# Row maxima of two heads in one instruction over two PSUM banks, with the diagonal's masks added by TensorE

## The reference

```python
scores = jnp.einsum('bqhd,bkhd->bhqk', Q, K) / math.sqrt(D_K)
causal = jnp.tril(jnp.ones((Sx, Sx), dtype=bool))
scores = jnp.where(causal, scores, -jnp.inf)
attn = jax.nn.softmax(scores, axis=-1)
out = jnp.einsum('bhqk,bkhd->bqhd', attn, V)
```

## Time and profile before

| | us |
|---|---|
| median of 3 runs | 2504.02 |
| lowest, highest | 2492.83, 2504.38 |
| the profiled execution | 2510.96 |
| its span, first to last instruction | 2509.3 |

### The profile page before, as it was taken

The page is one execution under the profiler, slowest core; times in us unless marked ns, Lnnn a source line. Parts: engine busy times, 40 slices in busy tenths (PEclk is TensorE's granted clock), DMA queues, the critical chain, the costliest instruction groups (busy, mean ns, idle before and its releaser), DMA issues. The chain is left out here.

```text
span 2509.3 us, 45515 instructions
## 1 busy us (share of the span) xinstructions
PE 2314.4 (92%) x16105; PEld 1323.9 (53%) x16105; DVE 1893.4 (75%) x5752; ACT 1516.1 (60%) x3189; POOL 505.8 (20%) x403
## 2 busy tenths in 40 slices
PE   5996999999999999999999999999957788999994
PEld 3553444444444444444444444444426688999994
DVE  3544988989989899899989988998707764666672
ACT  2541577778777778787777777787841102454451
POOL 0000001010110110101100100101005113777773
PEclk9996799989989899899989998998987787999997
DMA  5996405425244154253351551641117323666653
GB/s 166 295 243 194 57 5 70 52 36 70 37 52 61 19 75 54 29 70 43 45 70 26 63 61 19 78 52 28 15 34 223 127 84 103 141 132 136 143 124 85
DMA packets 145316, 214.56 MB, mean 86 GB/s; under 512 B 54560, under 2 KB 108000, under 8 KB 136672
## 3 DMA queue, kind: packets, MB, share of 16 engines
q1 hardware_dynamic: 132832, 195.27, 39.4%
q0 software_dynamic: 12288, 16.79, 5.2%
HBM read 138.43 MB, written 76.02 MB: 85 GB/s over the span
## 5 line engine op out<-in xcount | busy, mean ns | idle before, releaser
L654 ACT ACTIVATE probs<-s_banks 128x512 f32<-128x512 f32 (+3 forms) x2560 | 1184.6, 539 | 359.1 <-PE s_banks L605 200.6
L691 DVE TENSOR_REDUCE rowmax<-m_banks 128x1 f32<-128x512 f32 x1536 | 965.6, 682 | 87.5 <-PE m_banks L616 80.4
L605 PE MATMUL s_banks<-qs,ks 50*128 50x512 f32 (+3 forms) x2560 | 866.4, 437 | 15.7 <-ACT probs L654 9.5
L616 PE MATMUL m_banks<-ks,qs 48*128 48x512 f32 (+3 forms) x2560 | 830.6, 448 | 26.2 <-PEq L89 20.5
L634 PE MATMUL v_bank<-probs,vs 128*32 128x512 f32 (+3 forms) x5120 | 637.8, 572 | 1.0 <-ACT probs L654 0.4
L605 PEld LDWEIGHTS s_banks<-qs,ks 50*128 50x128 f32 x2560 | 422.2, 193 | 400.6 <-ACT probs L654 366.7
L616 PEld LDWEIGHTS m_banks<-ks,qs 48*128 48x128 f32 x2560 | 414.7, 197 | 297.3 <-DVE rowmax L691 137.5
L688 DVE CUSTOM_DVE_ANT_0 unused<-m_banks,c_maskq 128x128 bf16<-128x128 f32 (+3 forms) x1024 | 464.6, 486 | 81.1 <-issue 77.7
L551 POOL CAST nparts<-negmax 128x16 fp32r<-128x16 f32 x64 | 12.6, 197 | 1279.5 <-DVE negmax L697 1279.5
L1402 PE MATMUL e_banks<-w_parts,hid_parts 128*128 128x256 f32 x1536 | 188.8, 284 | 1.2 <-issue 0.5
L1402 PEld LDWEIGHTS e_banks<-w_parts,hid_parts 128*128 128x128 f32 x1536 | 185.4, 192 | 1.9 <-DVE hid_parts L1321 1.1
(11 more groups left out here) (181 smaller groups left out, 1823.8 us busy)
## 6 DMA issues: line engine op xcount, KB each, us to landing
w<-in_L_ffn_fc_w SPq DMA_DIRECT2D x32, 1024.0 KB, 5.2
qs<-q_scratch SPq DMA_DIRECT2D x96, 256.0 KB, 8.4
ks<-k_scratch SPq DMA_DIRECT2D x96, 256.0 KB, 10.2
q_scratch<-parts SPq DMA_DIRECT2D x64, 256.0 KB, 4.3
k_scratch<-parts SPq DMA_DIRECT2D x64, 256.0 KB, 4.5
v_scratch<-vt SPq DMA_DIRECT2D x16, 512.0 KB, 7.5
v_in<-v_scratch SPq DMA_DIRECT2D x32, 256.0 KB, 10.9
qs<-mrows SPq DMA_DIRECT2D x512, 2.0 KB
```

Source lines behind the costliest of these rows:

```text
L605: ins = pe.matmul(bank, ks[rows, slot, h // 2, k * P:(k + 1) * P], qs[rows, slot, h // 2, q * CH + first:(q + 1) * CH], start=True, stop=n ...
L616: pe.matmul(room(("M", NM * group + n))[:, 0:width], qs[rows, slot, h // 2, t * P:(t + 1) * P], ks[rows, slot, h // 2, c * CH:c * CH + wid ...
L654: act.activation(probs[:, n % PR, 0:width], s_banks[:, (NS * group + n) % SRING, 0:width], ACT.Exp, scale=SCALE).then_inc(p_ready, 1)
L691: dve.tensor_reduce(out, scores, AX.X, ALU.max).then_inc(m_used, 1)
```

## The change

The ring of four banks becomes a ring of two pairs: `m_banks` is [128, 2, 2, 512], `MRING` is 2, and a unit "M" is now the two blocks of the two halves that follow each other in `ROW_BLOCKS` (same rows, same columns, two heads). `group_order` appends a pair where it came to the second of its blocks. TensorE fills both banks, then on the diagonal adds the mask to each by two 64-column matmuls with an identity, as the score tiles do, and signals once. VectorE takes the maxima of both banks by one `tensor_reduce` with a [128, 2, width] input and a [128, 2] output, on the diagonal too; the masked instruction, its memset and `maskq` are gone. The transpose takes one of the two places of the ring (its first bank). Two bfloat16 tables come in, `later_row` and its copy with the halves swapped, with two more small DMAs.

```diff
--- before.py
+++ after.py
@@ -360,8 +360,8 @@
-            if group < G:
-                order.append(("M", group, n))
+            if group < G and n % 2 == 1:
+                order.append(("M", group, n // 2))
@@ -394,13 +394,14 @@
-MRING, SRING = 4, 3
+MRING, SRING = 2, 3
 ...
+    NP = NM // 2
@@ -411,7 +412,8 @@
-        ring.append(("M", block))
+        if block % 2 == 1:
+            ring.append(("M", block // 2))
@@ -434,10 +436,8 @@
-        unused = sb("unused", [P, GH, CH], BF16)
-        dve_pause = sb("dve_pause", [P, GH])
 ...
-        m_banks = ctx.enter_context(nc.psum_tensor("m_banks", [P, MRING, CH], F32))
+        m_banks = ctx.enter_context(nc.psum_tensor("m_banks", [P, MRING, 2, CH], F32))
@@ -581,7 +581,7 @@
-                while n >= 0 and ring[n][0] == "M" and ring[n][1] >= NM * G:
+                while n >= 0 and ring[n][0] == "M" and ring[n][1] >= NP * G:
@@ -608,16 +608,28 @@
-                        h, t, c = ROW_BLOCKS[n]
-                        width = min(CH, (t + 1) * P - c * CH)
 ...
-                        rows = slice(h % 2 * HALF, h % 2 * HALF + PAIR_ROWS)
-                        pe.matmul(room(("M", NM * group + n))[:, 0:width], qs[rows, slot, h // 2, t * P:(t + 1) * P],
-                                  ks[rows, slot, h // 2, c * CH:c * CH + width], start=True, stop=True).then_inc(m_ready, 1)
+                        banks = room(("M", NP * group + n))
+                        for half in range(2):
+                            h, t, c = ROW_BLOCKS[2 * n + half]
+                            width = min(CH, (t + 1) * P - c * CH)
+                            diagonal = c == t // TPC
+                            rows = slice(half * HALF, half * HALF + PAIR_ROWS)
+                            ins = pe.matmul(banks[:, half, 0:width], qs[rows, slot, h // 2, t * P:(t + 1) * P],
+                                            ks[rows, slot, h // 2, c * CH:c * CH + width], start=True, stop=not diagonal)
+                        if diagonal:
+                            for half in range(2):
+                                rows = slice(half * HALF, (half + 1) * HALF)
+                                for j in range(2):
+                                    mask = "later_row" if j == half else "later_row_swapped"
+                                    first = width - P + j * HALF
+                                    ins = pe.matmul(banks[:, half, first:first + HALF], const[mask][rows, :],
+                                                    const["identb"][rows, rows], start=False, stop=j == 1)
+                        ins.then_inc(m_ready, 1)
 ...
-                        bank = room(("N", turn))
+                        bank = room(("N", turn))[:, 0]
@@ -664,7 +676,7 @@
-                        act.activation(mrows[:, turn % 2, :], m_banks[0:PARTS * TILES, place[("N", turn)] % MRING, 0:P],
+                        act.activation(mrows[:, turn % 2, :], m_banks[0:PARTS * TILES, place[("N", turn)] % MRING, 0, 0:P],
@@ -678,20 +690,15 @@
-                        h, t, c = ROW_BLOCKS[n]
+                        h, t, c = ROW_BLOCKS[2 * n]
 ...
-                        out = rowmax[:, group % SLOTS, h % 2 * PAIRS + h // 2, t, c:c + 1]
-                        scores = m_banks[:, place[("M", NM * group + n)] % MRING, 0:width]
-                        dve.wait_ge(m_ready, NM * group + n + 1)
-                        if c == t // TPC:
-                            dve.memset(dve_pause[:, h:h + 1], 0.0)
-                            dve.tensor_tensor_reduce(unused[:, h, 0:width], scores, const["maskq"][:, CH - width:CH], 1.0, NEG,
-                                                     ALU.add, ALU.max, out).then_inc(m_used, 1)
-                        else:
-                            dve.tensor_reduce(out, scores, AX.X, ALU.max).then_inc(m_used, 1)
-                        if n in MAXIMA_ENDS:
-                            turn, q = NQ * group + MAXIMA_ENDS.index(n), t // TPC
-                            dve.wait_ge(m_used, NM * group + n + 1)
+                        out = rowmax[:, group % SLOTS, h // 2:h // 2 + PAIRS + 1:PAIRS, t, c]
+                        banks = m_banks[:, place[("M", NP * group + n)] % MRING]
+                        dve.wait_ge(m_ready, NP * group + n + 1)
+                        dve.tensor_reduce(out, banks[:, :, 0:width], AX.X, ALU.max).then_inc(m_used, 1)
+                        if 2 * n + 1 in MAXIMA_ENDS:
+                            turn, q = NQ * group + MAXIMA_ENDS.index(2 * n + 1), t // TPC
+                            dve.wait_ge(m_used, NP * group + n + 1)
@@ -1467,17 +1474,17 @@
-            for m in ("later_col",):
+            for m in ("later_col", "later_row"):
 ...
-            sp.wait_ge(swapped, 16 * 2)
+            sp.wait_ge(swapped, 16 * 4)
 ...
-            pool.memset(const["maskq"][:, :], 0.0)
+            pool.memset(const["later_row"][:, :], 0.0)
@@ -1493,8 +1500,8 @@
-            pool.affine_select(out=const["maskq"][:, CH - P:CH], in_=const["maskq"][:, CH - P:CH], compare_op=ALU.is_ge, fill=NEG, base=0,
-                               pattern=[[-1, P]], channel_multiplier=1).then_inc(made, 1)
+            pool.affine_select(out=const["later_row"][:, :], in_=const["later_row"][:, :], compare_op=ALU.is_ge, fill=NEG, base=0,
+                               pattern=[[1, P]], channel_multiplier=-1).then_inc(made, 1)
@@ -1524,9 +1531,9 @@
-                  "b1T": [P, E * F // P], "ident": [P, P], "upper": [P, P], "ones": [P, P], "eps": [P, 1], "maskq": [P, CH]}
+                  "b1T": [P, E * F // P], "ident": [P, P], "upper": [P, P], "ones": [P, P], "eps": [P, 1]}
 ...
-        for n in ("identb", "later_col", "later_col_swapped"):
+        for n in ("identb", "later_col", "later_col_swapped", "later_row", "later_row_swapped"):
```

## The result

The change takes 2695.03 us (median of 4 runs, 2692.02 to 2697.98) against 2498.67 us of the kernel before beside it (4 runs): ratio 1.0786 [1.075, 1.0822], 7.9% slower. The forecast was 2549 us, its upper bound 2612, and even the upper ends of all its terms together gave 2634. The sign was right, the size was not.

The account below looks back on a forecast made before the run. TensorE was taken as the nearer bound, VectorE 8 to 9 us a group behind. Terms 61 + 19 - 32 - 4 + 1 = +45 us gave 2556, or 2549 us against the median; own range 2517 to 2590, wider range 2472 to 2612.

Parts of the forecast that it names:

- In the plain run little changes: Plain pairs away from the transposes: issued with 1.1 us of reading ahead instead of 1.8, given no cost.
- Four banks as two pairs: Ring term: plain pairs cost nothing, but pairs behind transposes stop TensorE 0.3 us, four times a group, +19 us (0 to 51).
- I take 2 us a group: TensorE waits less for VectorE and pair halves stand side by side: -32 us (0 to -104).
- The count of TensorE, 90 of 92 us: TensorE's work in a stage B group, summed from starts: 90 us of the 92 to 94 at full clock.
- Masks: Diagonal pairs get four 64-column matmuls each on TensorE, 0.12 us a pair: +61 us (41 to 82).
- The transposes in the ring: Pair behind each transpose of the maxima waits for the pair ahead: 0.3 us of stopped TensorE, four a group, +19 us.
- 85 falling to 78: VectorE's work per group in us: each paired reduction saves 0.085 us, 6.8 a group, 109 us of VectorE in all.
- 76 to 80 us busy: Sign that the forecast is right: VectorE's busy time per group falls to this and it waits more for TensorE.
- 97 to 99 us: Sign that the forecast is right: fast groups take this long instead of 94 to 96 us.
- The lead-in: 88 blocks before stage B's first score tile, where VectorE hardly waits: 44 paired reductions save 4 us.
- Rival C: Two places too few also at 128- and 256-column pairs: another 2 to 4 us a group, about 2600 us, chance 0.12.
- Rival B: Clock falls where small masked tiles crowd: longer falls 2590 us, second falls 2650, chance 0.14; all short 2495, chance 0.06.

Follow-up runs that it names:

- e2: Kernel before with TensorE's blocks issued in twos at the place of the second, still four single banks: 2645.18 us, ratio 1.0627.
- e4: The change's ring of two pairs and order, but VectorE masks and reduces each pair by two instructions, with one release: 2690.78 us, ratio 1.0798 to the kernel before.
- e5: The change with all transposes of the maxima moved from the ring of pairs into the score tiles' ring: 2560.97 us, ratio 1.0321 to the kernel before.
- e1: The change without its 2048 mask matmuls, diagonal pairs reduced unmasked: 2533.98 us, ratio 1.0186 to the kernel before.
- e15: Kernel before with a ring of three single banks instead of four, nothing else changed: 2666.09 us, ratio 1.0734.
- e3: Kernel before with all row masks on TensorE and plain reductions, four single banks, old order: 2487.94 us, ratio 0.9998.
- e6: Kernel before with all transposes in the score tiles' ring, four single banks for the blocks alone: 2480.25 us, ratio 0.9996.

## Why the prediction was wrong

- **The failed step: "In the plain run little changes".** Under "Four banks as two pairs" the prediction named the plain pairs (1.1 us of reading ahead for 1.8) and put them at nothing; that a pair's halves "now always stand side by side" it even counted among the gains. The runs show here the largest cost. Order in twos alone is +4.1 us a group at full clock (e2), the ring of pairs on top +2.1 (e4). Of these 6.2 us the transposes are 1.7 by e5, so about 4.5 us a group, 72 us in all, stand where the sum had 0. The other two steps are one instruction for two, -1.3 (e1), and the masks, +3.3 (the change). The four add up to the whole by construction, as each is the difference of two neighbouring runs; that says nothing of another order of steps. In place of "little changes" TensorE waits more for ScalarE and VectorE more for TensorE, with four banks too (e2). Why the order in twos costs that is argued, not shown.
- **The second failed step: the clock.** It had no term in the sum, only a rival. It is 2.9 us a group, some 46 us. The first step and this one make 118 of the 146 us between forecast and result.
- **The gain of TensorE, "I take 2 us a group"**, was about right in size: VectorE's saving gives 1.3 (e1 against e4). That the reading ahead has a price here at all is shown by e15 (8.9 for one bank), though by another wait.
- **The count of TensorE, 90 of 92 us.** It was added from starts, some of which wait. The prediction took 0.34 us for two blocks of different halves from 1050.22 and 1050.56. The next two follow after 0.23:

```profile
1050.79 0.40 PE L605 MATMUL s_banks<-qs,ks 50*128 50x512 f32 x1
```

From 1050.22 to the product at 1051.12 three such twos take 0.90 us, 0.30 each. So the 38 us for 224 blocks are 34 by this place, and less if 0.23 is the price. "TensorE is the nearer bound" was read out of a sum with waits in it. That neither engine alone bounds fits the runs: 5.5 us less of VectorE bring 1.3 (e1), and the masks of 32 pairs more on TensorE cost 2.4 with single banks (e3), for the 3.8 foreseen.

- **Masks**: taken as 3.8 us a group (0.12 us a pair), measured 3.3 in the pairs and 2.4 in single banks: right in mechanism and nearly in size at full clock. With the clock's part, taking them out of the change saves 161 us (e1), for the 61 foreseen. The Trainium skill (TensorE: Matmul & The Clock Gate, "Wait — 56ns, not 53.3ns?") has a floor of about 25 ns from start to start. The two masks of one half start 0.04 us apart (1105.28 and 1105.32), in line with it, but the first two of the four masks of a pair start 0.01 us apart (1082.01 and 1082.02), below it; here the measurement decides. That these two are of different halves is inferred.
- **The transposes in the ring**: taken as 1.2 us a group, measured 1.7 (e5): the mechanism was right. What it did to the clock wasn't foreseen.
- **VectorE**: 83.4 us busy a group for 88.0; the prediction had 85 falling to 78 by starts, in 512-column pairs 1.12 us apart, and 3.49 us for three bears that out. Its mark, "76 to 80 us busy", set the count by starts against busy time and was missed. So was that of "97 to 99 us" for fast groups (102.5) and that of 0.12 to 0.20 us for four masks (0.07 where shown). Of 5.5 us saved on VectorE only 1.3 arrive, as it waits for TensorE anyway.
- **The lead-in**: -4 us foreseen; the first cast came at 263.92 us, before at 262.52. A saving on VectorE doesn't show there either.
- **Rival C, "the ring rules"**, had the right place and the wrong size: 2 to 4 us a group where e4 stands 6.2 above the kernel before, 4.1 of it by the order alone. Its mark, TensorE waiting over 25 us a group for VectorE, didn't come (8.5 us); a ring of three single banks came near it (24.0 us, e15). In the change it is VectorE that waits for TensorE.
- **Rival B, the clock**, came true in part, and beside the failed step. Long falls stand in 10 of 15 groups, hardly more than the nine before; but each fall, long or short, is some 6.5 us longer. The Trainium skill (same page, "A second HAM failure mode: psum-queue depth-cycling") tells of a kernel that cycled through PSUM banks and whose small pauses between groups of matmuls made the clock swing. The traces agree only in part. The falls do change with the ring: e5 loses them when only the transposes leave it. But e6 keeps them in a roomy ring, and e1 loses them in the small one.
- **The range** added each term's ends but put no price on the order in twos or on less depth. Each is a small edit of the kernel before (e2, e15), and nothing in the trace of before bounds what it costs.

**Open** are why the order in twos costs 4.1 us a group, and what decides whether the clock falls. No quantity that was varied (masks, order, depth, transposes) orders the runs. Nor was a deeper ring tried.

## What to carry to other kernels

Handing over two buffers at once changes the producer's order and halves the hand-overs that a ring holds, even if the bytes stay. Price both before the saved instructions, by two runs of the old kernel: one with the order in twos, one with a buffer fewer. A consumer that saves work gains little (1.3 of 5.5 us here) while the producer's order sets when its input is ready. If the clock moves from run to run, compare kernels by what they take at full clock too, and look at the clock of every execution, not of the traced one alone. A busy share near 100% on an engine whose row halves work side by side doesn't say that it has no waits.

## What was not expected of the hardware

- A slow microsecond at 1.2 GHz costs 0.36 to 0.38 us of time in the two kernels, about 0.4 in e2 (102.80 and 98.57 us for 10 us of it) and 0.39 over 59 executions of the kernel before, not the half that a group bound by TensorE's clock would lose.
- The falls come and go with edits that hardly change the work: e3 adds 2048 matmuls to the kernel before, its falls nearly vanish and its time stays.
- A maximum over two banks of 512 columns is 1.23 us long and follows the last at some 1.13 us (3.49 us for three), for 0.69 and 0.60 of a single one.
- Four 64-column matmuls on two row halves cover 0.07 us (1082.01 to 1082.08).
